# Edge rows gathered as pairs from a DRAM table built during the sort, results kept in place, bias products limited to the sort steps

## The chip, the cores and the metric

The kernel runs on one core of one Trainium2 chip. The metric is the device time of one execution in microseconds (us), as the median of several runs. The engines are TensorE (PE in the profile), VectorE (DVE), ScalarE (ACT), GpSimd (POOL) and SyncE (SP); SP's queue issues the plain DMAs and POOL's queue the indirect ones.

## The reference

A graph layer with residual and layer norm, on 50,000 nodes of 128 features and 12,500 edges of 128 features. `src` is drawn at random and unsorted.

```python
edge_sum = jax.ops.segment_sum(edge_attr, src, num_segments=50000)
inputs = jnp.concatenate([x, edge_sum], axis=1)          # 50000 x 256
h = jax.nn.elu(inputs @ W0 + b0)                         # W0 256 x 128
h = jax.nn.elu(h @ W2 + b2)                              # W2 128 x 128
y = x + h @ W3 + b3                                      # W3 128 x 128
m = jnp.mean(y, axis=-1, keepdims=True)
v = jnp.var(y, axis=-1, keepdims=True)
out = (y - m) / jnp.sqrt(v + 1e-05)
```

Everything is float32.

## The kernel before, in words

**Items.** The work is 124 items, numbered c. Items 0 to 97 (ND = 98) are dense: 512 nodes each, computed as if no edge touched them, and stored whole by plain DMAs. Items 98 to 122 (NE = 25, group g) are the edge items: 500 sorted edges each, as 4 columns of 125. Each takes the rows of x that its edges' sources name, adds the summed edge features in layer 1, and scatters its 500 result rows over what the dense items stored (rows that are not a node's last edge go out of bounds and are dropped). Item 123 (LAST) mends the sums that cross a column's end. So no scatter may start before all dense rows are stored.

**Steps.** Every engine walks the same steps c = 0 to 128, and in step c works on several items at once. TensorE: layer 1 of item c-1 (L487, for edge items also L498 with the sums), for edge items the transposes of x's rows (`turn`, L512), layer 2 of item c-2 (L519), layer 3 of item c-3 (L531 and L532, four blocks). ScalarE: exp of layer 1 (L591), the biased copy of x (L585), exp of layer 2 (L591), then `squares` of item c-3 (L600, L605, L607), whose result `seed` VectorE needs. VectorE: `root` of item c-4 (L832 to L838, waits for `seed`), elu of layer 1 (L819, L822), `normalise` of item c-4 (L850, its end counts `o_ready`), elu of layer 2. Each engine's queue is in order.

**Bias products.** Where `fused(s, layer)` holds, TensorE adds the bias by a short bf16 product (`add_bias`, L479), and VectorE's elu is one instruction (L815) and not two (L819, L822). It holds for both layers in the sort's steps 3 to 19, and for layer 2 in every even step from 20 to 98.

**Sort.** VectorE sorts the edges by source between its other work in steps 1 to 19 (KEY_AT = 20). SP then sends words and keys through DRAM. From step 21 POOL knows the sorted edge numbers (`edge_i`) and sources (`key_i`).

**Gathers.** POOL issues 4 indirect DMAs for the features of group g (L369, 125 rows of 512 bytes each) and 4 for its rows of x (L375), 200 in all; `pace` spreads them over the dense items by waiting on `o_ready`.

**Sums.** In steps 95 to 119 (`SUMS`, group g in step 95 + g) TensorE multiplies the features by 0/1 masks (`sums`, L463, four products, one behind each part of its step), and ScalarE copies the sum out of PSUM (`copy_sums`, L574) at the end of its step, behind `squares`. The first product of the next group waits for that copy (`sum_ready`). VectorE makes the masks (L788) of the next group from `keyB`, the keys of one group spread over 128 partitions.

**SP's order.** In step c SP issues the load of item c+3, then waits for `o_ready` of item c-4 and stores it if it is dense. In steps 95 to 115 it also issues `load_keys(g+4)` (L322), which waits until the masks of group g are made, since `keyB` has four slots.

**End.** When SP's stores have landed (POOL itself waits on the four `stored` semaphores), POOL scatters: 4 indirect DMAs for each edge item (L391), each item when `o_ready` says so, and one for LAST (L384).

Of the kernel before, what the change touches and what calls it, by code (L numbers as in the profile page):

```python
# [12 lines left out]
P = 128  # L13
J = 4
# [9 lines left out]
def gnn_resnorm(nc, x, src, attr, W0, b0, W2, b2, W3, b3, x_items, word_rows, key_rows, out):  # L24
# [22 lines left out]
    LAST = ND + NE  # L47
    NI = LAST + 1
    SLOTS = 4
    SUM_SLOTS = 5  # L50
    AHEAD = 3

# [27 lines left out]
    KEY_AT = SORT_AT + len(GROUPS)  # L80
    SUM_LEAD = 3
    SUMS = {ND - SUM_LEAD + g: g for g in range(NE)}
# [3 lines left out]
    assert KEY_AT + 2 < min(SUMS) and END_AT <= LAST  # L86

    with ExitStack() as ctx:
# [76 lines left out]
        attr_edge = sb("attr_edge", [P, EC, P])  # L165
        x_edge = sb("x_edge", [P, EC, P])
# [70 lines left out]
        attr_got = [sem(f"attr_got{k}") for k in range(SLOTS)]  # L237
        x_got = [sem(f"x_got{k}") for k in range(SLOTS)]
        x_loaded = [sem(f"x_loaded{k}") for k in range(SLOTS)]
        stored = [sem(f"stored{k}") for k in range(SLOTS)]  # L240
        scattered = [sem(f"scattered{k}") for k in range(SLOTS)]

        DENSE_ON = [len(range(k, ND, SLOTS)) for k in range(SLOTS)]
# [9 lines left out]
        def is_dense(c):  # L253
            return c < ND
# [6 lines left out]

        def scatters(c):

            return 16 * sum(blocks(k) for k in range(ND, c + 1) if k % SLOTS == c % SLOTS)
# [26 lines left out]
        def _(sp):  # L291
# [9 lines left out]
            def rows_of(ap, c):  # L301
                first = N - ROWS if c == ND - 1 else c * ROWS
                return ap[first:first + ROWS, :].rearrange("(p j) f -> p (j f)", p=P)

            def load(c):
                if not is_dense(c):
                    return
                k = c % SLOTS
                at_least(sp, xT_ready, c - SLOTS + 1)
                sp.dma_start(x_sb[:, k, :], x_items[c * P:(c + 1) * P, :]).then_inc(x_loaded[k], 16)  # L310

            def store(c):
                sp.wait_ge(o_ready, c + 1)
                if c == ND - 1:

                    sp.wait_ge(stored[(c - 1) % SLOTS], 16 * DENSE_ON[(c - 1) % SLOTS])
                sp.dma_start(rows_of(out, c), o_sb[:, c % SLOTS, :]).then_inc(stored[c % SLOTS], 16)
# [10 lines left out]
            for c in range(STEPS_END):  # L328
# [5 lines left out]
                load(c + AHEAD)  # L334
                if 0 <= c - 4 < ND:
                    store(c - 4)
# [9 lines left out]
            for k in range(SLOTS):  # L346
                sp.wait_ge(stored[k], 16 * DENSE_ON[k])

        @block.gpsimd
        def _(pool):  # L350
# [6 lines left out]
            def pace(half):  # L357

                first = KEY_AT - 1
                pool.wait_ge(o_ready, first + half * (ND - 6 - first) // (2 * NE))  # L360

            def gather(g):
                k = g % SLOTS
                pace(2 * g)
                if g >= SLOTS:
                    pool.wait_ge(attr_got[k], got(g - SLOTS))
                    pool.wait_ge(x_got[k], got(g - SLOTS))
                for c in range(J * g, J * g + J):
                    nc.gpsimd.indirect_dma_start(  # L369
                        out=attr_edge[0:EP, c, :], out_offset=None, in_=attr[:, :],  # L370
                        in_offset=bass.IndirectOffsetOnAxis(ap=edge_i[0:EP, c:c + 1], axis=0),
                    ).then_inc(attr_got[k], 16)
                pace(2 * g + 1)
                for c in range(J * g, J * g + J):
                    nc.gpsimd.indirect_dma_start(  # L375
                        out=x_edge[0:EP, c, :], out_offset=None, in_=x[:, :],
                        in_offset=bass.IndirectOffsetOnAxis(ap=key_i[0:EP, c:c + 1], axis=0),
                    ).then_inc(x_got[k], 16)

            def scatter_out(c):  # L380
                k = c % SLOTS
# [544 lines left out]
```

## Time and profile before

| | before |
|---|---|
| median of 3 runs | 605.97 us (605.18 to 607.83) |
| the profiled execution, its own time | 606.39 us |
| its span, first to last instruction | 604.3 us |
| TensorE busy | 544.3 us, 90% |
| VectorE busy | 466.1 us, 77% |
| ScalarE busy | 439.7 us, 73% |
| GpSimd busy | 371.9 us, 62% |
| DMA bytes | 77.84 MB, mean 129 GB/s |

The span leaves 606.39 - 604.3 = 2.1 us of the execution outside. Busy shares are means over stages that differ: the sort (to some 108 us), the dense steps (to some 395 us), the steps with sums (to some 550 us), and a tail. A wait matters only where the waiting engine sets the time of its stage.

### The profile page before, as it was taken

To read this page: it belongs to the slowest core of one execution; us is meant where nothing else is said; L and a number is where in the kernel's file an instruction comes from. 1 tells how busy PE (TensorE), PEld (TensorE's weight loads), DVE (VectorE), ACT (ScalarE), POOL (GpSimd) and SP (SyncE) were. 2 spreads that over 40 slices of the span, in tenths; PEclk is the share of its full clock that TensorE was granted. 3 is DMA by queue.
4 is the path that set the end of the run, shared out by engine and by line. 5 is a ranking of instruction groups with operands and counts; after the bars stand their busy time and mean duration, and the time that the engine had idled before them with its cause. 6 is when DMAs were issued, how large, how long until landed. Compare 5 with 4: busy or idle time off the path is not lost.

```text
span 604.3 us, 10977 instructions
## 1 busy us (share of the span) xinstructions
PE 544.3 (90%) x2930; PEld 360.4 (60%) x2930; DVE 466.1 (77%) x1348; ACT 439.7 (73%) x1632; POOL 371.9 (62%) x310
## 2 busy tenths in 40 slices
PE   3999999999999999999999999989999999997930
PEld 1455555566666666666666666666667666665620
DVE  5988899988888888888888888877678676776640
ACT  2577767888888888888888988876665666665630
POOL 0000000377887787788778778877157777777676
PEclk9999999999999999999999999999999999999985
DMA  3134332486666655555665656554422332211111
GB/s 111 49 109 120 121 106 91 144 245 184 183 180 183 180 175 179 178 174 175 181 180 183 175 174 179 173 153 117 112 77 76 82 79 71 71 38 37 34 39 34
DMA packets 57451, 77.84 MB, mean 129 GB/s; under 512 B 22590, under 2 KB 27782, under 8 KB 57390
## 3 DMA queue, kind: packets, MB, share of 16 engines
q1 hardware_dynamic: 33294, 58.26, 31.7%
q0 software_dynamic: 24096, 18.89, 12.7%
q8 instruction: 24, 0.39, 0.3%
q14 instruction: 37, 0.30, 0.2%
HBM read 45.30 MB, written 32.24 MB: 128 GB/s over the span
## 4 chain that ended last, share of the span: by engine, by line
PE 82%; DVE 9%; issue 5%; POOL 2%; ACT 1%; SPq 0%; DMA 0%; DVEq 0%; POOLq 0%
PE z_ps L531 18%; PE z_ps L532 17%; PE l_ps L519 17%; PE l_ps L487 16%; PE sum_ps L463 5%; PE l_ps L498 4%; PE l_ps L479 3%; PE turn_ps L512 2%; POOL out_dram L391 2%; DVE h L815 2%; DVE net L721 2%; DVE o_sb L850 1%; DVE net L720 1%; PE turn_ps L435 1%; DVE e L819 0%
## 5 line engine op out<-in xcount | busy, mean ns | idle before, releaser
L369 POOL DMA_INDIRECT attr_edge<-in_edge_attr_dram,edge_i x100 | 124.8, 1248 | 143.9 <-issue 141.1
L531 PE MATMUL z_ps<-center,xT 128*128 128x128 f32 (+1 forms) x986 | 194.7, 279 | 8.5 <-issue 6.4
L600 ACT ACTIVATE sq<-z_ps 128x128 f32<-128x128 f32 (+1 forms) x493 | 129.8, 278 | 94.7 <-PE z_ps L532 93.7
L532 PE MATMUL z_ps<-w3c,h 128*128 128x128 f32 (+1 forms) x986 | 190.1, 274 | 0.0
L531 PEld LDWEIGHTS z_ps<-center,xT 128*128 128x128 f32 (+1 forms) x986 | 152.3, 191 | 41.5 <-issue 36.3
L391 POOL DMA_INDIRECT out_dram<-o_sb,target_i x100 | 119.9, 1199 | 53.5 <-issue 49.3
L532 PEld LDWEIGHTS z_ps<-w3c,h 128*128 128x128 f32 (+1 forms) x986 | 149.0, 191 | 0.0
L375 POOL DMA_INDIRECT x_edge<-in_x_dram,key_i x100 | 124.3, 1243 | 30.5 <-issue 28.1
L822 DVE SCALAR_TENSOR_TENSOR h<-l_ps,neg_bias,e 128x512 f32<-128x512 f32 (+2 forms) x174 | 129.2, 742 | 6.2
L519 PE MATMUL l_ps<-h,w 128*128 128x512 f32 (+1 forms) x248 | 130.0, 606 | 1.8 <-DVE h L822 1.8
L591 ACT ACTIVATE e<-l_ps,bias 128x512 f32<-128x512 f32 (+2 forms) x174 | 116.7, 671 | 18.7 <-issue 5.3
L487 PE MATMUL l_ps<-xT,w0x 128*128 128x512 f32 (+1 forms) x248 | 128.8, 601 | 1.2 <-ACT xT L585 1.2
L600 ACT ACTIVATION_READ_ACCUMULATOR sq<-z_ps 128x1 f32 (+1 forms) x493 | 102.0, 207 | 0.0
L819 DVE TENSOR_SCALAR e<-e,bias 128x512 f32<-128x512 f32 (+2 forms) x174 | 95.6, 550 | 3.8 <-issue 2.5
L850 DVE TENSOR_TENSOR o_sb<-z_ps,rstd 128x512 f32<-128x512 f32 (+1 forms) x124 | 84.1, 678 | 0.1
L585 ACT ACTIVATE xT<-x_sb,bias_x 128x512 f32<-128x512 f32 x98 | 69.8, 712 | 7.6 <-DVE neg_bias L668 7.6
L519 PEld LDWEIGHTS l_ps<-h,w 128*128 128x128 f32 x248 | 43.7, 192 | 44.1 <-issue 29.8
L463 PEld LDWEIGHTS sum_ps<-same,attr_edge 125*128 125x128 f32 x200 | 31.8, 190 | 42.9 <-issue 41.7
L832 DVE SCALAR_TENSOR_TENSOR newton<-seed 128x4 f32<-128x4 f32 (+1 forms) x124 | 20.7, 167 | 45.1 <-ACT seed L607 44.3
L591 ACT ACTIVATE e<-l_ps,minus_one 128x512 f32<-128x512 f32 x74 | 49.9, 675 | 4.4 <-PE l_ps L479 3.8
L463 PE MATMUL sum_ps<-same,attr_edge 125*128 125x125 f32 x200 | 39.9, 283 | 12.7 <-issue 12.7
L815 DVE SCALAR_TENSOR_TENSOR h<-e,l_ps 128x512 f32<-128x512 f32 x74 | 50.2, 679 | 0.0
(126 smaller groups left out, 402.5 us busy)
## 6 DMA issues: line engine op xcount, KB each, us to landing
x_sb<-x_items_dram SPq DMA_DIRECT2D x98, 256.0 KB
out_dram<-o_sb SPq DMA_DIRECT2D x98, 256.0 KB
keyB<-key_rows_dram SPq DMA_DIRECT2D x25, 250.0 KB
attr_edge<-in_edge_attr_dram,edge_i POOLq DMA_INDIRECT x100
x_edge<-in_x_dram,key_i POOLq DMA_INDIRECT x100
out_dram<-o_sb,target_i POOLq DMA_INDIRECT x100
w<-in_L_gnn_W_dram SPq DMA_DIRECT2D x2, 64.0 KB, 1.9
w0x<-in_L_gnn_W_dram SPq DMA_DIRECT2D x1, 64.0 KB, 2.1
```

What stands on the lines that cost most here:

```text
L369: nc.gpsimd.indirect_dma_start(out=attr_edge[0:EP, c, :], out_offset=None, in_=attr[:, :], in_offset=bass.IndirectOffsetOnAxis(ap=edge_i[0 ...
L375: nc.gpsimd.indirect_dma_start(out=x_edge[0:EP, c, :], out_offset=None, in_=x[:, :], in_offset=bass.IndirectOffsetOnAxis(ap=key_i[0:EP, c: ...
L391: nc.gpsimd.indirect_dma_start(out=out[:, :], out_offset=bass.IndirectOffsetOnAxis(ap=target_i[0:EP, col:col + 1], axis=0), in_=o_sb[0:EP, ...
L463: T.matmul(sum_ps[:, j * EP:(j + 1) * EP], attr_edge[0:EP, c, :], same[0:EP, c % (2 * J), :], start=True, stop=True).then_inc(same_free, 1)
L487: mm = T.matmul(ps, w0x[:], xT[:, c % SLOTS, 0:n], start=True, stop=alone)
L519: mm = T.matmul(l2_ps[c % 2][:, 0:n], w2[:], h1[:, c % 2, 0:n], start=True, stop=not fused(s, 2))
L531: T.matmul(z, xT[:, c % SLOTS, j * q:(j + 1) * q], center[:], start=True, stop=False)
L532: mm = T.matmul(z, h2[:, c % 2, j * q:(j + 1) * q], w3c[:], start=False, stop=True)
L591: A.activation(e[:, c % 2, 0:n], ps[:, 0:n], ACT.Exp, bias=bias[:, 0:1]).then_inc(done, 1)
L600: t = A.activation(sq[0:q, j, :], z_ps[c % 2][0:q, j * P:(j + 1) * P], ACT.Square, scale=float(P) ** -0.5, accum_out=ssq[0:q, c % 2, j:j + 1])
L819: V.tensor_scalar(e[:, c % 2, 0:n], e[:, c % 2, 0:n], 1.0, bias[:, 0:1], ALU.min, ALU.add).then_inc(min_ready, 1)
L822: V.scalar_tensor_tensor(out=h[:, c % 2, 0:n], in0=ps[:, 0:n], scalar=neg_bias[:, 0:1], in1=e[:, c % 2, 0:n], op0=ALU.max, op1=ALU.add).th ...
```

## The change

Five things change.

1. While VectorE sorts, a table `pairs` of 12,500 rows of 256 floats is built in DRAM: the row of x of the edge's source in the left half, the edge's features in the right. POOL fetches the x rows of the unsorted edges (`fetch_x`, 100 indirect DMAs, starting as soon as `src` is in), SP writes them to the table (`pair_x`, 25 DMAs in steps 2, 3, 5, 6, ... 38) and copies the features from DRAM to DRAM (`pair_attr`, 25 DMAs in steps 2 to 26).
2. After the sort POOL gathers pairs, 100 indirect DMAs of 125 rows of 1024 bytes in place of 200 of 512 bytes, without `pace`, once all 25 pieces of both halves have landed.
3. `normalise` writes an edge item's rows over its x rows in `pair_edge`, and the scatters read them there; the wait for earlier scatters is gone.
4. POOL waits for one count, `dense_out`, in place of the four `stored` semaphores. SP raises it by one for each dense item (`confirm`): for item d-2 behind the store of item d, and for items 96 and 97 behind the last step of its loop.
5. `fused` holds only in steps 3 to 19. `sums` puts two products behind layer 1 and two behind `turn`. `copy_sums` stands ahead of `squares`.

```diff
+    PAIR_X = {2 + 3 * g // 2: g for g in range(NE)}
+    PAIR_ATTR = {2 + g: g for g in range(NE)}
...
         def fused(s, layer):
-            if s < KEY_AT:
-                return FUSED_FROM <= s
-            return layer == 2 and s % 2 == 0 and is_dense(s - 2)
+            return FUSED_FROM <= s < KEY_AT
...
+            def confirm(d):
+                sp.wait_ge(stored[d % SLOTS], 16 * (d // SLOTS + 1))
+                sp.sem_inc(dense_out, 1)
+
+            def pair_x(g):
+                k = g % SLOTS
+                sp.wait_ge(x_fetched[k], 16 * J * (g // SLOTS + 1))
+                sp.dma_start(pairs.rearrange("(p c) f -> p c f", p=EP)[:, J * g:J * g + J, 0:P],
+                             x_early[0:EP, k, :, :]).then_inc(x_paired[k], 16)
+
+            def pair_attr(g):
+                last = min(E, ROWS * (g + 1))
+                sp.dma_start(pairs[ROWS * g:last, P:2 * P], attr[ROWS * g:last, :]).then_inc(attr_paired, 16)
...
+                if item_in(c - 4) and is_dense(c - 4):
+                    d = ITEMS[c - 4][1]
+                    store(d)
+                    if d >= 2:
+                        confirm(d - 2)
+                if c in PAIR_ATTR:
+                    pair_attr(PAIR_ATTR[c])
+                if c in PAIR_X:
+                    pair_x(PAIR_X[c])
...
                 if c in SUMS and SUMS[c] + SLOTS < NE:
                     load_keys(SUMS[c] + SLOTS)
-            for k in range(SLOTS):
-                sp.wait_ge(stored[k], 16 * DENSE_ON[k])
+            confirm(ND - 2)
+            confirm(ND - 1)
...
+            def fetch_x(g):
+                k = g % SLOTS
+                at_least(pool, x_paired[k], 16 * (g // SLOTS))
+                for j in range(J):
+                    nc.gpsimd.indirect_dma_start(
+                        out=x_early[0:EP, k, j, :], out_offset=None, in_=x[:, :],
+                        in_offset=bass.IndirectOffsetOnAxis(ap=src_i[0:EP, J * g + j:J * g + j + 1], axis=0),
+                    ).then_inc(x_fetched[k], 16)
...
+            pool.wait_ge(src_loaded, 16)
+            for g in range(NE):
+                fetch_x(g)
+            for k in range(SLOTS):
+                pool.wait_ge(x_paired[k], 16 * len(range(k, NE, SLOTS)))
+            pool.wait_ge(attr_paired, 16 * NE)
             pool.wait_ge(edge_ready, 1)
             for g in range(NE):
                 gather(g)
...
             pool.wait_ge(target_ready, 1)
-            for k in range(SLOTS):
-                pool.wait_ge(stored[k], 16 * DENSE_ON[k])
-            for c in range(ND, NI):
-                scatter_out(c)
+            pool.wait_ge(dense_out, ND)
+            for g in range(NE):
+                scatter_out(g)
...
-                return [one(j) for j in range(J)]
+                return [some(0), some(1)]
...
+                if c in SUMS:
+                    parts.append(lambda: copy_sums(SUMS[c]))
                 if item_in(c - 3):
                     parts.append(lambda: squares(c - 3))
                 run(parts, [])
-                if c in SUMS:
-                    copy_sums(SUMS[c])
...
+                elif kind == "edge":
+                    rows_out = pair_edge[0:EP, J * n:J * n + J, 0:P]
```

SP's queue at its end, before the change (the last dense stores, then `load_keys` L322 alone; the last row is the end, with its waits for the stores):

```order
L317 DMA out_dram<-o_sb 128x512 [waits o_ready]
L322 DMA keyB<-key_rows_dram 128x500 [waits same_ready]
L317 DMA out_dram<-o_sb 128x512 [waits stored0,o_ready]
L322 DMA keyB<-key_rows_dram 128x500 [waits same_ready] x15
L88 UNCONDITIONAL_BRANCH [waits stored2,stored3,stored1,stored0]
```

The same place after the change. The two waits on the last row are those of `confirm(96)` and `confirm(97)`, which raise `dense_out` to 98:

```order
L341 DMA keyB<-key_rows_dram 128x500 [waits stored2,same_ready]
L321 DMA out_dram<-o_sb 128x512 [waits stored0,o_ready]
L341 DMA keyB<-key_rows_dram 128x500 [waits stored3,same_ready]
L341 DMA keyB<-key_rows_dram 128x500 [waits same_ready] x14
L100 UNCONDITIONAL_BRANCH [waits stored0,stored1]
```

The last loads of keys (15 before, and 15 after in two rows) stood behind the last dense store before and still do; what moved is that the count which releases POOL is now raised behind them. POOL's queue after the change, from the last gather of pairs (L398) over the row for LAST (L421) to the first scatters (L406), shows who waits:

```order
L398 DMA pair_edge<-pairs_dram,edge_i 125x256 x3
L421 DMA x_end<-in_x_dram,end_i 100x128 [waits ends_ready]
L406 DMA out_dram<-pair_edge,target_i 50000x128 [waits o_ready,dense_out,target_ready]
L406 DMA out_dram<-pair_edge,target_i 50000x128 x3
L406 DMA out_dram<-pair_edge,target_i 50000x128 [waits o_ready]
```

The first scatter waits for `dense_out`, and all others are queued behind it.

TensorE in one step with sums, before the change (L463 are the products of the sums, L512 the transposes of `turn`):

```order
L498 MATMUL l_ps<-sumT,w0e 128x500 [waits sum_ready]
L463 MATMUL sum_ps<-same,attr_edge 128x125 [waits same_ready,sum_ready,attr_got3]
L512 MATMUL turn_ps<-ident,x_edge 128x125 [waits xT_ready,x_got0]
L512 MATMUL turn_ps<-ident,x_edge 128x125 x3
L463 MATMUL sum_ps<-same,attr_edge 128x125 [waits same_ready]
L519 MATMUL l_ps<-h,w 128x500 [waits h2_ready,h1_ready]
L463 MATMUL sum_ps<-same,attr_edge 128x125 [waits same_ready]
L531 MATMUL z_ps<-center,xT 125x128 [waits o_ready,h2_ready]
```

And ScalarE in the same step before, from the copy at a step's end on:

```order
L574 COPY sumT<-sum_ps 128x500 [waits parts_ready,l1_ready,same_free]
L591 ACTIVATE e<-l_ps,bias 128x500 [waits h1_ready,l1_ready]
L585 ACTIVATE xT<-turn_ps,bias_x 128x500 [waits z_ready,turn_ready]
L591 ACTIVATE e<-l_ps,bias 128x500 [waits h2_ready,l2_ready]
L600 ACTIVATE sq,ssq<-z_ps 125x128 [waits ssq_ready,rstd_ready,z_ready]
L600 ACTIVATE sq,ssq<-z_ps 125x128 x3
L605 ACTIVATE seed<-ssq,eps 125x4 [waits ssq_ready]
L607 ACTIVATE seed<-seed 125x4 [waits log_ready]
```

TensorE after the change, the same step:

```order
L523 MATMUL l_ps<-sumT,w0e 128x500 [waits sum_ready]
L488 MATMUL sum_ps<-same,pair_edge 128x125 [waits same_ready,sum_ready,pair_got3]
L488 MATMUL sum_ps<-same,pair_edge 128x125 [waits same_ready]
L537 MATMUL turn_ps<-ident,pair_edge 128x125 [waits xT_ready,pair_got0]
L537 MATMUL turn_ps<-ident,pair_edge 128x125 x3
L488 MATMUL sum_ps<-same,pair_edge 128x125 [waits same_ready] x2
L544 MATMUL l_ps<-h,w 128x500 [waits h2_ready,h1_ready]
L556 MATMUL z_ps<-center,xT 125x128 [waits o_ready,h2_ready]
```

ScalarE after it:

```order
L599 COPY sumT<-sum_ps 128x500 [waits parts_ready,l1_ready,same_free]
L626 ACTIVATE sq,ssq<-z_ps 125x128 [waits ssq_ready,rstd_ready,z_ready]
L626 ACTIVATE sq,ssq<-z_ps 125x128 x3
L631 ACTIVATE seed<-ssq,eps 125x4 [waits ssq_ready]
L633 ACTIVATE seed<-seed 125x4 [waits log_ready]
L617 ACTIVATE e<-l_ps,bias 128x500 [waits h1_ready,l1_ready]
```

All four products now stand ahead of layers 2 and 3, and the copy stands ahead of `squares`, which waits for layer 3.

## Rows read from the trace of the kernel before

**Rows 1.** Page: span, TensorE's busy time, the chain that ended last

```profile
span 604.3 us, 10977 instructions
PE 544.3 (90%) x2930; PEld 360.4 (60%) x2930; DVE 466.1 (77%) x1348; ACT 439.7 (73%) x1632; POOL 371.9 (62%) x310
PE 82%; DVE 9%; issue 5%; POOL 2%; ACT 1%; SPq 0%; DMA 0%; DVEq 0%; POOLq 0%
```

**Rows 2.** L322 (SP's loads of keys): ns min/median/max, first and last start us

```profile
L322 SPq DMA_DIRECT2D keyB<-key_rows_dram x25: 319/320/655, 123.8 to 518.3; - x25
```

**Rows 3.** L391 (POOL's scatters), and POOL's last two: start us, us, operation

```profile
L391 POOL DMA_INDIRECT out_dram<-o_sb,target_i x100: 1186/1190/1407, 443.0 to 598.5; - x100
...
598.49 1.19 POOL L391 DMA_INDIRECT out_dram<-o_sb,target_i  x1 [0.30 <-issue]
599.98 0.99 POOL L384 DMA_INDIRECT out_dram<-o_sb,end_i  x1 [0.30 <-issue]
```

**Rows 4.** Timeline: VectorE's L850 for items 17, 90, 98 and 110

```profile
108.56 0.68 DVE L850 TENSOR_TENSOR o_sb<-z_ps,rstd 128x512 f32<-128x512 f32 x1
...
394.61 0.68 DVE L850 TENSOR_TENSOR o_sb<-z_ps,rstd 128x512 f32<-128x512 f32 x1
...
441.23 0.69 DVE L850 TENSOR_TENSOR o_sb<-z_ps,rstd 125x512 f32<-125x512 f32 x1
...
516.03 0.68 DVE L850 TENSOR_TENSOR o_sb<-z_ps,rstd 125x512 f32<-125x512 f32 x1
```

**Rows 5.** Source view of POOL's gathers of features, L369

```profile
L369 POOL DMA_INDIRECT attr_edge<-in_edge_attr_dram,edge_i x100: 1208/1212/1427, 115.2 to 417.8; - x100
```

**Rows 6.** Timeline of two dense steps: the rows of one loop through three engines

```profile
247.18 0.28 ACT L600 ACTIVATE sq<-z_ps 128x128 f32<-128x128 f32 x1 [0.79 <-PE z_ps L532]
...
248.92 0.17 DVE L832 SCALAR_TENSOR_TENSOR newton<-seed 128x4 f32<-128x4 f32 x1 [1.05 <-ACT seed L607]
...
252.05 0.75 DVE L822 SCALAR_TENSOR_TENSOR h<-l_ps,neg_bias,e 128x512 f32<-128x512 f32 x1
...
252.85 0.49 PE L531 MATMUL z_ps<-center,xT 128*128 128x128 f32 x2 [0.17 <-issue]
...
254.94 0.28 ACT L600 ACTIVATE sq<-z_ps 128x128 f32<-128x128 f32 x1 [0.79 <-PE z_ps L532]
```

**Rows 7.** The chain, same steps: start us, us, what

```profile
250.65 0.86 PE l_ps L487 x2
251.50 0.86 PE l_ps L519 x2
252.36 0.32 PE l_ps L479
252.68 0.17 issue
252.85 0.49 PE z_ps L531 x2
253.34 0.22 PE z_ps L532 x2
```

**Rows 8.** Timeline of a step with sums: the copy and the product behind it

```profile
480.56 1.01 PE L487 MATMUL l_ps<-xT,w0x 128*128 128x500 f32 x2
...
482.16 0.56 ACT L574 COPY sumT<-sum_ps 128x500 f32<-128x500 f32 x1
...
482.82 0.46 PE L463 MATMUL sum_ps<-same,attr_edge 125*128 125x125 f32 x2 [0.41 <-issue]
...
486.79 1.01 PE L487 MATMUL l_ps<-xT,w0x 128*128 128x500 f32 x2
```

**Rows 9.** Windows: us, busy PE, PEld, DVE, ACT, POOL, clock, DMA share, GB/s

```profile
60.00:90.00 30.00, 29.30 (x150) 16.96 (x150) 27.31 (x120) 21.91 (x81) 0.00 (x0) 1.00 0.38 119
...
120.00:135.00 15.00, 14.62 (x82) 10.15 (x82) 12.57 (x31) 11.73 (x47) 12.26 (x10) 1.00 0.82 244
```

**Rows 10.** DMA queues: POOL's queue, packets, MB, share of 16 engines

```profile
q0 software_dynamic: 24096, 18.89, 12.7%
```

More of the change, by code:

```diff
@@ L51, in gnn_resnorm @@
     AHEAD = 3
+    ITEMS = [("dense", d) for d in range(ND)] + [("edge", g) for g in range(NE)]
+    LAST = len(ITEMS)
+    ITEMS.append(("last", 0))
+    NI = len(ITEMS)
+    DENSE_AT = [c for c in range(NI) if ITEMS[c][0] == "dense"]
+    EDGE_AT = [c for c in range(NI) if ITEMS[c][0] == "edge"]
+    assert [ITEMS[c][1] for c in DENSE_AT] == list(range(ND)) and [ITEMS[c][1] for c in EDGE_AT] == list(range(NE))
     LOG = 7
@@ L80, in gnn_resnorm @@
     KEY_AT = SORT_AT + len(GROUPS)
+    PAIR_X = {2 + 3 * g // 2: g for g in range(NE)}
+    PAIR_ATTR = {2 + g: g for g in range(NE)}
     SUM_LEAD = 3
-    SUMS = {ND - SUM_LEAD + g: g for g in range(NE)}
+    SUMS = {EDGE_AT[g] - SUM_LEAD: g for g in range(NE)}
     END_AT = max(SUMS) + 2
@@ L85, in gnn_resnorm @@
     FUSED_FROM = 3
-    assert KEY_AT + 2 < min(SUMS) and END_AT <= LAST
+    assert max(PAIR_X) + 4 < min(SUMS) and KEY_AT + 5 < min(SUMS) and END_AT <= LAST
     with ExitStack() as ctx:
@@ L253, in is_dense @@
         def is_dense(c):
-            return c < ND
+            return ITEMS[c][0] == "dense"
         def item_in(c):
@@ L404, in _ @@
             pool.wait_ge(target_ready, 1)
-            for k in range(SLOTS):
-                pool.wait_ge(stored[k], 16 * DENSE_ON[k])
-            for c in range(ND, NI):
-                scatter_out(c)
-            for c in range(NI - SLOTS, NI):
-                pool.wait_ge(scattered[c % SLOTS], scatters(c))
+            pool.wait_ge(dense_out, ND)
+            for g in range(NE):
+                scatter_out(g)
+            pool.wait_ge(o_ready, LAST + 1)
+            nc.gpsimd.indirect_dma_start(
+                out=out[:, :], out_offset=bass.IndirectOffsetOnAxis(ap=end_i[0:EC, 1:2], axis=0),
+                in_=x_end[0:EC, :], in_offset=None, bounds_check=N - 1, oob_is_err=False,
+            ).then_inc(scattered, 16)
+            pool.wait_ge(scattered, 16 * (EC + 1))
         @block.tensor
@@ L455, in sums, with some @@
             def sums(g):
-                def one(j):
+                def some(half):
                     def do():
-                        c = J * g + j
-                        if j == 0:
-                            pe.wait_ge(attr_got[g % SLOTS], got(g))
+                        if half == 0:
+                            pe.wait_ge(pair_got[g % SLOTS], got(g))
                             at_least(pe, sum_ready, g)
-                        pe.wait_ge(same_ready, c + 1)
-                        T.matmul(sum_ps[:, j * EP:(j + 1) * EP], attr_edge[0:EP, c, :], same[0:EP, c % (2 * J), :],
-                                 start=True, stop=True).then_inc(same_free, 1)
+                        for j in range(2 * half, 2 * half + 2):
+                            c = J * g + j
+                            pe.wait_ge(same_ready, c + 1)
+                            T.matmul(sum_ps[:, j * EP:(j + 1) * EP], pair_edge[0:EP, c, P:2 * P], same[0:EP, c % (2 * J), :],
+                                     start=True, stop=True).then_inc(same_free, 1)
                     return do
@@ L510, in turn @@
                 for j in range(blocks(c)):
-                    rows_in = x_end[0:q, :] if c == LAST else x_edge[0:q, J * (c - ND) + j, :]
+                    rows_in = x_end[0:q, :] if c == LAST else pair_edge[0:q, J * ITEMS[c][1] + j, 0:P]
                     mm = T.transpose(turn_ps[:, j * q:(j + 1) * q], rows_in, ident[0:q, 0:q])
```

114 lines of the change are left out of this document (46 added, 68 removed).

## The prediction

> **What bounds the kernel now.** I read the page first. TensorE is busy 90% of the 604.3 us span and the chain that ended last runs over it for 82% [rows 1], so TensorE, or a loop that contains it, sets most of the time. The exception is the end. POOL's scatters start at 443.0, the last of item 122 at 598.49 and LAST's at 599.98, 1.49 us apart, without a wait for anything but issue [rows 3]. The reader should see there that 100 such scatters need 100 x 1.49 = 149 us, whatever the other engines do, and that they begin right behind the dense stores. Third I read SP's row of key loads: the last is issued at 518.3 [rows 2], 75 us after the scatters began. Last the timelines of a dense step and of a step with sums, for the loops through several engines.
>
> **The release of the scatters.** The edit that decides is the fourth. Before, POOL itself waited for the stores. After, it waits for `dense_out` = 98, and the last two counts are raised by SP behind its whole loop, behind `load_keys(24)`. That load waits until the masks of group 20 are made, in step 114. Before, nobody waited for SP there; now the first scatter does, and behind it in POOL's queue all 101. In the old schedule the load goes out at 518.3 and takes 0.3, so the release would come at 518.6 [rows 2]. Item 98's output ended at 441.23 + 0.69 = 441.9 and the first scatter began at 443.0 [rows 3, 4]: 1.1 us from release to scatter. So with all else unmoved: 518.6 + 1.1 + 149 + 0.99 for LAST + 3.3 from its end (600.97) to the span's end (604.3) = 673.0. Compute ends long before (LAST's rows come near 585 or earlier), so nothing hides this, and everything that the change gains counts only up to step 114. The scatter itself costs what it did: 125 rows of 512 bytes, another source tile. Bounds of its pace: 1.49, or 1.71 if each took the longest 1.41 beside busy engines; 40 of them run beside compute, and the median of 1.19 over all, most of them beside compute [rows 3], speaks for 1.49.
>
> **Dense steps: bias products.** 37 of the 40 products removed lie in steps 20 to 94. In the chain one costs 0.32, and 0.17 of issue and a first block of 0.49 where the next takes 0.22 follow it [rows 7]: 0.76 us, or 37 x 0.76 = 28 us if TensorE alone set the steps. I do not believe that. Follow the loop [rows 6]: ScalarE starts its squares at 247.18, VectorE's root begins on their result at 248.92 (+1.74), VectorE works without a pause to the end of L822 at 252.80 (+3.88), TensorE starts layer 3 at 252.85, and the squares after it start at 254.94 (+2.09). That closes in 7.76 us for two steps, and items 17 to 90 came every (394.61 - 108.56) / 73 = 3.92 us [rows 4], 7.84 for two. So the pair is set by the step in which VectorE has both elus in two instructions; the step with the bias product is the one with slack. After the change both kinds of steps are the long kind, and both loops close in 7.76, or 7.49 if a block's restart (0.27) goes. VectorE alone needs 3.55 to 3.88 a step. I take 3.85 where it was 3.92: 75 x 0.07 = 5 us gained. Bounds: 28 gained (above), 5 lost if two tight loops disturb each other.
>
> **Steps with sums.** Before, the copy out of PSUM starts at 482.16, behind the squares, and TensorE's first product of the next group at 482.82, after a wait of 0.41 [rows 8]. Layer 3, squares, copy and the next product form a loop of one step, and the step is 486.79 - 480.56 = 6.23 us [rows 8]. After, the copy no longer waits for layer 3. TensorE's own work is then 3 x 0.86 for the wide products, 8 x 0.22 in layer 3, 4 x 0.22 for the sums and 0.44 for the transposes = 5.66, by the pieces of [rows 7], so 0.57 less in each of 16 steps, 9 us. Steps 95 to 98 still hold dense items and little else and can gain another 3. Together 12 us before step 114; bounds 5 (half of it is lost to restarts) and 14.
>
> **The sort, and the table.** POOL was idle there. A gather takes 1.21 [rows 5] and with the issue gap of 0.3 some 1.5, so `fetch_x` needs 150 us; `pair_x(24)` goes out in step 38, near 108.6 + 17 x 3.9 = 175 us [rows 4]. The pair gathers then run from 180 to some 335, and the first sum needs them near 385: hidden, with 50 us to spare. If that cover went, each us late would be a us. The traffic: pieces of 256 KB, of x fetched every 6 us and written every 7.1, of features copied once a step of 4.8, add 43 + 36 + 55 = 134 GB/s to 119, that is 253 [rows 9]. The stretch 120 to 135 moved 244 GB/s at a share of 0.82 with TensorE busy 97% [rows 9]. So I take 2 us. Lower bound 0; the upper one is the third rival. SP's extra issues (50 in 36 steps, at some 0.4 each) lie in its waits. Halving POOL's gathers after the sort gains nothing, since they were hidden.
>
> **The sum.** 673.0 - 5 - 12 + 2 = 658 us of span. The profiled execution had 2.1 us outside its span, 606.39 in all, 0.4 above the median of the runs: 658 + 2.1 - 0.4 = 660 us.
>
> **The rivals.**
>
> 1. *TensorE alone bounds the dense steps.* For it: the chain names TensorE only. Against: the loop above. The 28 us come off in full instead of 5: 637. Chance 0.1.
>
> 2. *The count is not late* (the other side). If `dense_out` were full when the last dense store lands, the first scatter would start near 443.0 - 5 - 3 = 435 and the end be 435 + 149 + 0.99 + 3.3 + 2.1 - 0.4 = 590: faster by 2.6%. It is one mechanism: the place of the last two `confirm`. The point from which it decides is a release at 606 - 156 = 450 us; the key load stands at 518.3 before the gains of 15 us [rows 2]. The queue order leaves no way around it, unless I misread what that load waits for. Chance 0.03.
>
> 3. *The table's traffic stretches the sort.* `pair_x` has 125 partitions. If its 256,000 bytes went over only 5 of the 16 engines, each would get 51 KB. POOL's queue moved 18.89 MB in 12.7% of 16 x 604.3 us, 15.4 KB a us and engine [rows 10], so 3.3 us each. On those engines the shares in the sort are 0.38 as before [rows 9], 0.22 for the features (1.06 of 4.8 us), 0.17 for the fetch and 3.3 / 7.1 = 0.46: 1.23, and as much up to step 38. Over 180 us that overfills by up to 28 us, and loads and stores in SP's queue come late with it: 686. Spread over all 16 it is 0.91, and the 2 us above hold. The trace has no row of a single engine; a mean share of 0.38 is no proof that 1.23 would be needed. Chance 0.17. The Trainium skill states it, in "DMA: Bandwidth & Descriptors", "Why a DMA increments its semaphore by 16 and not by 1": a transfer runs on the largest number of engines, at most 16, that divides the sizes of both slowest dimensions, for 125 that is 5. By that rule alone the sum would be 686, by the rows of the mean share 660; but the page's own figure of about 27 GB/s for an engine would leave room for it. No row here shows either.
>
> **How the numbers follow.** My forecast has 0.68 (range of its own 650 to 670), the rivals 0.1, 0.03 and 0.17, and 0.02 is for what I do not see. A range that leaves out 2 in 10 must reach toward the third rival, whose middle is 675: 644 to 680. A measurement of this kernel tells 0.5% from no change, 3 us. Only the second rival is not slower: slower 0.96, same 0.01, faster 0.03.
>
> **What would show it.** After: the last key load near 500 us, the first scatter 1 to 2 us behind it and no scatter before; some 100 scatters 1.49 apart with TensorE idle in the last 90 us; dense steps of 3.8 to 3.9 without alternation; steps with sums of 5.7; the copy ahead of the squares; pair gathers from 180 to 335; item 17 near 109 us. I am wrong if scatters begin near 440, if the dense steps fall to 3.5, or if item 17 comes later than 115.

## The result, and the profile after

| | before | after |
|---|---|---|
| median | 605.76 us (605.18 to 607.83, 4 runs) | 674.02 us (672.65 to 678.45, 4 runs) |
| ratio | 1 | 1.1134, 95% interval 1.1106 to 1.1163 |
| span of the profiled execution | 604.3 us | 670.9 us |

The kernel is 68 us slower. The page of the changed kernel: span, busy times, two of the slices, the chain that ended last.

```profile
span 670.9 us, 11033 instructions
...
PE 529.9 (79%) x2890; PEld 358.4 (53%) x2890; DVE 483.5 (72%) x1388; ACT 439.2 (65%) x1632; POOL 372.5 (56%) x310
...
PE   3999998889999999999999999999999969200000
...
POOL 7866676657728888888880000000004777778676
...
PE 37%; DVE 19%; issue 15%; POOL 12%; ACT 10%; DMA 4%; another core or an unknown queue 2%; SPq 1%; POOLq 0%; ACTq 0%; DVEq 0%
```

A slice is 16.8 us. TensorE is idle in the last five, and POOL stands idle in nine slices while all others work; then it runs alone to the end. In [rows 1] TensorE carried 82% of the chain, here 37%. The source view of SP's last key load and of POOL's scatters, and the timeline of the hand-over, which answer to [rows 2, 3]:

```profile
L341 SPq DMA_DIRECT2D keyB<-key_rows_dram x25: 319/320/2834, 132.2 to 509.8; - x25
```

```profile
L406 POOL DMA_INDIRECT out_dram<-pair_edge,target_i x100: 1185/1189/1332, 511.3 to 664.7; - x100
```

```profile
509.82 0.32 SPq L341 DMA_DIRECT2D keyB<-key_rows_dram  x1
...
511.30 1.33 POOL L406 DMA_INDIRECT out_dram<-pair_edge,target_i  x1 [157.24 <-issue]
...
666.15 0.99 POOL L430 DMA_INDIRECT out_dram<-x_end,end_i  x1 [0.30 <-issue]
```

The load ends at 510.1 and the first scatter begins 1.2 us later. POOL had been idle for 157 us; the releaser reads "issue", so the profile names nobody for this wait; what released POOL has to be read from the code and from SP's row. From 511.3 to LAST's row at 666.15 are 154.9 us for 100 scatters, 1.55 each.

VectorE's output of an item is the kernel's clock; its starts (for item 98 and 110 the edge rows) in us, before against after, with the differences over each stretch:

| item | before | after | stretch | before | after |
|---|---|---|---|---|---|
| 30 | 161.18 | 168.07 | start to 30 | 161.18 | 168.07 |
| 90 | 394.61 | 401.62 | 30 to 90 | 233.43 | 233.55 |
| 98 | 441.23 | 440.53 | 90 to 98 | 46.62 | 38.91 |
| 110 | 516.03 | 507.56 | 98 to 110 | 74.80 | 67.03 |

So the first 30 items cost 6.9 us, the 60 dense ones gained nothing, and the steps with sums gained 15.5 us. All of it counts only through the release of POOL. A few us of one trace are not a result by themselves: four kernels below that run the same code up to step 19 (the changed one, e1, e2, e4) have item 17 at 112.72, 115.09, 111.38 and 109.57.

The two dense steps in the timeline after, to hold against [rows 6]:

```profile
256.56 0.49 PE L556 MATMUL z_ps<-center,xT 128*128 128x128 f32 x2 [0.57 <-DVE h L848]
...
258.64 0.28 ACT L626 ACTIVATE sq<-z_ps 128x128 f32<-128x128 f32 x1 [0.87 <-PE z_ps L557]
...
260.38 0.16 DVE L858 SCALAR_TENSOR_TENSOR newton<-seed 128x4 f32<-128x4 f32 x1 [0.46 <-ACT seed L633]
...
263.57 0.75 DVE L848 SCALAR_TENSOR_TENSOR h<-l_ps,neg_bias,e 128x512 f32<-128x512 f32 x1
264.38 0.49 PE L556 MATMUL z_ps<-center,xT 128*128 128x128 f32 x2 [0.54 <-DVE h L848]
```

The bias product is gone, and in its place TensorE waits 0.57 and 0.54 us for VectorE's `h`. The pair takes 264.38 - 256.56 = 7.82 us, as before (7.76 to 7.84).

### The profile page after: what moved, and what is told of

Its sections match the earlier page's. It is cut to its first block, busy times and chain, and to the rows that moved or that the text cites. A ratio compares the mean times of both kernels' runs of the same rounds, so it can differ in the third digit from the quotient of the medians.

```text
span 670.9 us, 11033 instructions
## 1 busy us (share of the span) xinstructions
PE 529.9 (79%) x2890; PEld 358.4 (53%) x2890; DVE 483.5 (72%) x1388; ACT 439.2 (65%) x1632; POOL 372.5 (56%) x310
## 4 chain that ended last, share of the span: by engine, by line
PE 37%; DVE 19%; issue 15%; POOL 12%; ACT 10%; DMA 4%; another core or an unknown queue 2%; SPq 1%; POOLq 0%; ACTq 0%; DVEq 0%
PE z_ps L556 10%; PE z_ps L557 9%; POOL out_dram L406 9%; ACT sq L626 6%; PE l_ps L544 5%; DVE e L845 5%; PE l_ps L512 5%; DVE h L848 4%; PE sum_ps L488 3%; POOL x_early L388 3%; PE l_ps L523 3%; ACT seed L631 2%; DMA pairs_dram<-x_early 2%; PE turn_ps L537 1%
## 5 line engine op out<-in xcount | busy, mean ns | idle before, releaser
L406 POOL DMA_INDIRECT out_dram<-pair_edge,target_i x100 | 119.3, 1193 | 192.5 <-issue 191.9
L848 DVE SCALAR_TENSOR_TENSOR h<-l_ps,neg_bias,e 128x512 f32<-128x512 f32 (+1 forms) x214 | 159.1, 744 | 7.6
L617 ACT ACTIVATE e<-l_ps,bias 128x512 f32<-128x512 f32 (+1 forms) x214 | 143.4, 670 | 24.4 <-PE l_ps L544 13.3
L388 POOL DMA_INDIRECT x_early<-in_x_dram,src_i x100 | 123.7, 1237 | 57.4 <-DMA pairs_dram<-x_early 28.1
L398 POOL DMA_INDIRECT pair_edge<-pairs_dram,edge_i x100 | 126.5, 1265 | 43.4 <-issue 30.2
L512 PE MATMUL l_ps<-xT,w0x 128*128 128x512 f32 (+1 forms) x248 | 130.4, 608 | 6.3 <-ACT xT L611 4.7
L845 DVE TENSOR_SCALAR e<-e,bias 128x512 f32<-128x512 f32 (+1 forms) x214 | 111.4, 521 | 8.3 <-ACT e L617 4.4
L879 DVE TENSOR_TENSOR o_sb<-z_ps,rstd 128x512 f32<-128x512 f32 x98 | 66.7, 681 | 0.0
L858 DVE SCALAR_TENSOR_TENSOR newton<-seed 128x4 f32<-128x4 f32 (+1 forms) x124 | 19.7, 159 | 58.7 <-ACT seed L633 43.5
L512 PEld LDWEIGHTS l_ps<-xT,w0x 128*128 128x128 f32 x248 | 38.6, 196 | 9.0 <-ACT xT L611 5.9
L631 ACT ACTIVATE seed<-ssq,eps 128x4 f32<-128x4 f32 (+1 forms) x124 | 36.8, 297 | 4.0
L488 PE MATMUL sum_ps<-same,pair_edge 125*128 125x125 f32 x200 | 31.2, 276 | 0.6 <-issue 0.3
```

Of the source, the lines that this page charges most:

```text
L388: nc.gpsimd.indirect_dma_start(out=x_early[0:EP, k, j, :], out_offset=None, in_=x[:, :], in_offset=bass.IndirectOffsetOnAxis(ap=src_i[0:EP ...
L398: nc.gpsimd.indirect_dma_start(out=pair_edge[0:EP, c, :], out_offset=None, in_=pairs[:, :], in_offset=bass.IndirectOffsetOnAxis(ap=edge_i[ ...
L406: nc.gpsimd.indirect_dma_start(out=out[:, :], out_offset=bass.IndirectOffsetOnAxis(ap=target_i[0:EP, c:c + 1], axis=0), in_=pair_edge[0:EP ...
L488: T.matmul(sum_ps[:, j * EP:(j + 1) * EP], pair_edge[0:EP, c, P:2 * P], same[0:EP, c % (2 * J), :], start=True, stop=True).then_inc(same_f ...
L512: mm = T.matmul(ps, w0x[:], xT[:, c % SLOTS, 0:n], start=True, stop=alone)
L617: A.activation(e[:, c % 2, 0:n], ps[:, 0:n], ACT.Exp, bias=bias[:, 0:1]).then_inc(done, 1)
```

## The experiments

Ratios are against the kernel before, run beside each experiment; its median was 604.48 us beside e1 to e4, 603.66 beside e5 to e8, 605.50 beside e9 to e11 and 604.64 beside e12. Between these groups the ratios are the safer measure.

**e1: the count is raised early.** The changed kernel, with the last two counts raised in step 102, ahead of that step's key load:

```diff
+                if c == ND + 4:
+                    confirm(ND - 2)
+                    confirm(ND - 1)
                 if c in SUMS and SUMS[c] + SLOTS < NE:
                     load_keys(SUMS[c] + SLOTS)
-            confirm(ND - 2)
-            confirm(ND - 1)
```

> The changed kernel with the last two counts raised at the top of step 102, right behind the last dense store's step, and not behind SP's whole loop. My theory (the late count costs all of the loss): the dense rows land near 441, the first scatter starts near 442.5, and from there to the end it takes what it took in the changed kernel, 670.9 - 511.3 = 159.6 us: span 602, 605 us. Rival (the table or the pair gathers also cost something behind the release): the span stays above 620.

Measured: 604.79 us, ratio 0.9998 (0.9978 to 1.0019), span 604.3. The source view of its scatters:

```profile
L407 POOL DMA_INDIRECT out_dram<-pair_edge,target_i x100: 1185/1189/1354, 443.8 to 598.1; - x100
```

The whole loss is gone by moving two lines. What else the change does adds up to nothing in the time; e3 and what follows show that this nothing is a gain and a loss.

**e2: the same lines in step 108.** A dose between the two: `if c == ND + 10`, the rest as in e1.

> The changed kernel with the last two counts raised at the top of step 108, behind the key loads for group 16 (which wait for the masks of group 12). My theory: the release follows that load, near 465, and the end follows the release by the same 160.8 us (510.1 to 670.9): span 626, 629 us. Rival (the late end has another cause, such as the queue's depth or the source tile of the scatters): no change from 674, or a time not in line with the release.

Measured: 627.15 us, ratio 1.0377 (1.0345 to 1.0408), span 625.9.

```profile
L407 POOL DMA_INDIRECT out_dram<-pair_edge,target_i x100: 1185/1188/1417, 465.4 to 619.7; - x100
```

First scatter at 443.8, 465.4 and 511.3 in e1, e2 and the changed kernel; from there to the end of the span 160.5, 160.5 and 159.6 us. The time is the release and a constant.

**e3: the sums' part alone.** The kernel before, with two products behind layer 1 and two behind `turn`, and the copy ahead of `squares`:

```diff
-                return [one(j) for j in range(J)]
+                return [some(0), some(1)]
...
+                if c in SUMS:
+                    parts.append(lambda: copy_sums(SUMS[c]))
                 if item_in(c - 3):
                     parts.append(lambda: squares(c - 3))
                 run(parts, [])
-                if c in SUMS:
-                    copy_sums(SUMS[c])
```

> The kernel before with one part of the change: two products of the sums behind layer 1 and two behind the transposes, and the copy ahead of the squares. My theory (one loop per step through layer 3, squares, copy and the first product): steps with sums fall from 6.25 to 5.6 us, item 98 ends 7.5 us earlier, the first scatter starts near 435.5 and the scatters, now behind compute all the time, end the span near 597: 599 us, 1.1% faster. Rival (VectorE or TensorE holds the step at 6.2 anyway): 606, steps of 6.2.

Measured: 595.72 us, ratio 0.9851 (0.981 to 0.9892). Item 98 at 435.08 against 441.23, and its first scatter at 436.8 against 443.0: the 6 us by which the dense items end earlier. From there to the end of the span it takes 158.1 us, against 604.3 - 443.0 = 161.3 before, so another 3 us come from behind item 98. Before, an item of four scatters had to wait for its rows, which came every 6.23 us, where four scatters need 4 x 1.49 = 5.96. The first scatter of item 99 in the kernel before shows it:

```profile
447.51 1.24 POOL L391 DMA_INDIRECT out_dram<-o_sb,target_i  x1 [0.30 <-issue]
449.20 1.19 POOL L391 DMA_INDIRECT out_dram<-o_sb,target_i  x1 [0.45 <-issue]
```

Item 99's output ends at 448.29, about 1 us ahead of that scatter, as with item 98. In e3 items 98 to 110 come every 6.02 us (5.6 was expected), and most of these waits are gone.

**e4: bias products back.** e1 with `fused` as before.

> e1_confirm_early with the bias products of the even steps put back (40 more products, the one other difference). My theory (a loop of VectorE, layer 3 and squares sets two dense steps): item 90 ends within 2 us of e1, the time is within 2 us of e1. Rival (TensorE alone sets the dense steps, and the gain was hidden by the table's traffic): item 90 ends some 28 us later and the time is some 28 us longer than e1.

Measured: 603.71 us, ratio 1.0005 (0.9976 to 1.0034). Items 30 to 90 took 233.1 us (e1 232.3). The 40 products cost nothing in the time. Item 90 came 4.2 us earlier than in e1, not within 2; but at item 17, up to where the two kernels run the same code, it was 5.5 us ahead already.

**e5: bias products out, without the table.** e3 with `fused` as in the change.

> e3 (the kernel before with the new order of sums and copy) without the bias products of the even steps: no table, the old gathers. My theory (the loop sets the dense steps): items 30 to 90 take 233 us as in e3, the time is within 2 us of e3, 596. Rival (the products cost TensorE 0.76 each, and the table's traffic hid that gain in the changed kernel): item 90 ends up to 28 us earlier, 570.

Measured: 596.6 us, ratio 0.9868 (0.9841 to 0.9895), the same as e3. Its item 30 comes at 162.62 and item 98 at 438.07, and items 30 to 90 took 235.5 us where 233 was expected: without the products the dense steps are, if anything, longer. Its scatters:

```profile
L389 POOL DMA_INDIRECT out_dram<-o_sb,target_i x100: 1185/1189/1393, 439.8 to 588.9; - x100
```

These 100 start 149.1 / 99 = 1.51 us apart. In e1 it was 154.3 / 99 = 1.56; this difference is taken up below.

**e6 and e7: VectorE's output behind layer 2.** In e6 (e3 otherwise, products kept) and e7 (e5 otherwise, without them), to shorten VectorE's part of the loop:

```diff
-                run([scale, first_layer, output, second_layer], beside)
+                run([scale, first_layer, second_layer, output], beside)
```

> e3 with VectorE's output of item c-4 put behind the elu of layer 2 instead of ahead of it, bias products of the even steps kept. My theory: the loop through VectorE gets 0.6 shorter (7.16 for two steps), but TensorE with one product in two steps needs 2 x 3.51 + 0.76 = 7.78, so the steps stay at 3.9: within 3 us of e3. Rival (VectorE's order is without effect on any bound): the same; a gain of over 8 us would speak against the price of 0.76.

> e6 without the bias products of the even steps. My theory: the loop is 7.16 for two steps and TensorE needs 7.02, VectorE 3.55 to 3.7 a step, so dense steps take some 3.65 and not 3.89: item 90 ends some 18 us earlier than in e3, and the tail of scatters with it: 578. Rival (VectorE or ScalarE alone holds 3.9 once all steps have two-instruction elus): 595, as e3.

Measured: e6 591.94 us, ratio 0.978 (0.9748 to 0.9812), the best of all kernels here, 3.8 us below e3 where at most 3 was expected; e7 596.24, ratio 0.9863 (0.9836 to 0.989), where 578 was expected. The windows of e6 show TensorE without a gap:

```profile
200.00:250.00 50.00, 49.88 (x274) 33.92 (x274) 41.82 (x99) 44.70 (x173) 39.94 (x34) 1.00 0.64 183
```

In e7, one of two steps shows what the sum had missed:

```profile
256.09 0.68 DVE L849 TENSOR_TENSOR o_sb<-z_ps,rstd 128x512 f32<-128x512 f32 x1
...
256.92 0.46 PE L530 MATMUL z_ps<-center,xT 128*128 128x128 f32 x2 [0.51 <-DVE o_sb L849]
```

Layer 3 writes into one of two `z_ps` buffers, and it waits until the output has read the older one. With the output last and without the products, two steps still take 7.76 us; with the products (e6) they take 7.58. As a reading of this row: a missing bias product gives TensorE 0.5 us only to wait; where the product stands, it fills that wait and makes VectorE's step shorter by an instruction. In this order the products are a gain (items 30 to 90 in 228.0 us against 233.3), where in the old order they made no difference.

**e8: the table's x half in two transfers.** e1, with `pair_x` cut into 112 and 13 partitions; the same bytes. POOL's two waits for these transfers count 32 a piece in place of 16 (left out here).

```diff
-                sp.dma_start(pairs.rearrange("(p c) f -> p c f", p=EP)[:, J * g:J * g + J, 0:P],
-                             x_early[0:EP, k, :, :]).then_inc(x_paired[k], 16)
+                for low, high in ((0, 112), (112, EP)):
+                    sp.dma_start(pairs.rearrange("(p c) f -> p c f", p=EP)[low:high, J * g:J * g + J, 0:P],
+                                 x_early[low:high, k, :, :]).then_inc(x_paired[k], 16)
```

> e1_confirm_early with each DMA that writes x rows into the table cut into one of 112 partitions and one of 13. Theory of the third rival (125 partitions go over 5 of the 16 engines, and that delays the table and what stands behind it): POOL's waits for these DMAs (28 us in 8 waits, and 13 before the first pair gather) fall below 8 and 5, item 17 ends near 109 to 110, the time is 0 to 4 us below e1. Rival (the sheer bytes of the table slow the sort): waits, item 17 (110 to 115) and time as in e1.

Measured: 599.27 us, ratio 0.9916 (0.9886 to 0.9947), 5.5 us below e1 (0.8% by the ratios; the slowest run of e8, 600.55, is below the fastest of e1, 601.61). Item 17 at 109.82 against 115.09, item 30 at 163.35 against 170.82. POOL's waits for these transfers fell from 30.8 us in e1 to 19.7, and the one before the first gather of pairs from 12.3 to 8.1; below 8 and below 5 were expected. SP's queue in the timeline, first of e1, then of e8:

```profile
103.85 0.62 SPq L331 DMA_DIRECT2D pairs_dram<-x_early  x1
104.52 2.71 SPq L314 DMA_DIRECT2D x_sb<-x_items_dram  x1
```

```profile
98.80 1.17 SPq L332 DMA_DIRECT2D pairs_dram<-x_early  x2
100.01 0.40 SPq L314 DMA_DIRECT2D x_sb<-x_items_dram  x1
```

Behind a `pair_x` of 125 partitions, the issue of the next load holds SP for 2.71 us; behind the two pieces for 0.40. Over all 23 loads that stand right behind a `pair_x`, the median is 2.92 us in the changed kernel and 0.44 in e8. The stretch 60 to 90 us in windows, first of the changed kernel, then of e8:

```profile
60.00:90.00 30.00, 29.28 (x143) 16.27 (x143) 26.66 (x113) 21.73 (x87) 20.50 (x18) 1.00 0.82 230
```

```profile
60.00:90.00 30.00, 29.24 (x143) 16.23 (x143) 27.02 (x117) 21.80 (x83) 19.79 (x18) 1.00 0.83 240
```

The mean share of the engines and the bytes are the same or higher, so more traffic is not what made e1 slower than e8. That the slow issues made it is not shown: e4 has them too (median 3.17) and its item 17 at 109.57, as early as e8's.

**e9, e10, e11: VectorE's root behind layer 1.** With `run([first_layer, scale, output, second_layer], beside)`, in e5 (e9), e3 (e10) and e8 (e11), to take the root out of the loop of [rows 6].

> e3 without the bias products of the even steps, and with VectorE's root of item c-4 moved from ahead of the elu of layer 1 to behind it. e7 had put the output, which layer 3 waits for too (two z buffers), in the place of the elu in the same loop: 3.81 of VectorE either way. Here the wait for the seed stands behind 1.2 us of other work, so the loop loses 1.2 us of its 7.76. My theory, mended: TensorE needs 3.51 a step and VectorE 3.55 to 3.65, dense steps of 3.6; items 30 to 90 take 216 and not 233, the end moves 20 to 23 us: 573 to 576. Rival (VectorE at 3.9 a step by its own work, or ScalarE at 3.5 with its waits): 595.

> e9 with the bias products of the even steps kept. In e6 TensorE ran without a gap, and two steps took 7.59 = 2 x 3.51 + 0.57. My theory: the same here, 3.80 a step, 592 us; so the products cost nothing as long as the loop stands (e4, e5) and some 0.2 a step, 15 to 20 us in all, once it is gone. Rival (products free of cost): as e9.

> The whole change with three mends: the last two counts raised in step 102 (e1), the writes of x rows cut in 112 and 13 partitions (e8), root behind the elu of layer 1 (e9). My theory: e8's 599 less the 20 to 23 us of the dense steps: 577 to 580, so the table still costs some 3 us against e9 and brings nothing. Rival (with half the gathers VectorE and POOL disturb each other less, so it ends ahead of e9): 570.

Measured: e9 619.43 us, ratio 1.0229 (1.0183 to 1.0275); e10 618.79, ratio 1.0228 (1.0197 to 1.0258); e11 625.58, ratio 1.0354 (1.0298 to 1.0411). All three went the wrong way. A row of e9:

```profile
253.09 0.52 DVE L818 TENSOR_SCALAR e<-e,bias 128x512 f32<-128x512 f32 x1 [0.75 <-ACT e L590]
```

VectorE now stands still for ScalarE's exp of layer 1. ScalarE is in order: that exp comes behind the squares and the seed. The root had used this wait; behind the elu it became 0.6 us of work in the loop. By this row the last link of the loop into VectorE is the exp, not the seed.

**e12: all together.** e8 with the bias products back and e6's order.

> The changed kernel with the count raised early and the table written in two transfers (599.27 us), its even-step bias products put back, and VectorE's order in a dense step as in the best version of the kernel before: scale, first layer, second layer, output (591.94 us there, against 595.72 us with the output ahead of the second layer, both with the products kept). If the loop of the dense steps sets the middle here as it does there, the pair of dense steps falls from 7.8 to 7.6 us with 30 to 40 pairs behind it, so 599.3 less 4 to 7 us: 593 to 595 us, and the table of pairs is then a cost of 1 to 3 us that buys nothing. Rival: 100 gathers fewer relieve the dense steps once TensorE bounds them, and the time is 590 us or less.

Measured: 602.98 us (600.69 to 604.43, 10 runs), ratio 0.9968 (0.995 to 0.9986): 3.7 us slower than e8, where 5 faster was expected. Item 17 comes at 112.29 (e8 109.82), items 30 to 90 take 230.8 us (e8 232.6, e6 228.0), and 90 to 98 take 41.3 (e8 38.9, e6 41.9). So against e8 this kernel gains 1.8 us in the dense steps and loses 2.4 behind item 90, 2.5 by item 17 and 0.5 from there to item 30. Item 16 still stands where it stood (106.47 against 106.39). In the next step a row of the timeline has TensorE waiting for the sorted words:

```profile
111.63 0.35 PE L468 MATMUL turn_ps<-ident,words 100*125 100x100 f32 x1 [2.31 <-DMA words<-word_rows_dram]
```

In e8 the same wait is 0.41. The transfer took about as long in both, 2.9 us from its issue to this row against 2.6, so the row says where the step lost time and not that the table's traffic did it. Both expectations failed. Against e6, which has no table, this kernel is 1.9% slower.

## Why the prediction was right in direction and 14 us short

**How much of it was luck.** The main mechanism was forecast and is shown. The number 660 was 14 us short, and the forecast's own range of 650 to 670 missed 674. The stated 644 to 680 holds it only because it was stretched toward the third rival, which did not come at its size. The misses also cancelled in part: 4.9 us more in the sort, 5.1 less gained in the dense steps and 5.9 more in the scatters, against 3.5 more gained in the steps with sums.

**The release of the scatters: right.** The last key load, the first scatter 1.2 us behind it, no scatter before, TensorE idle in the last five slices, 84 us: all as forecast, and e1 and e2 show by dose that this alone makes the 68 us. The second rival (the count is not late) fell with it; its 590 would have needed more than an early count, since e1, which makes the count early, gives 604.8: the first scatter there starts at 443.8 and not at 435. The release came at 510.1 and not at 518.6 - 15 = 503.6, and the scatters took 154.9 us and not 149. The span's miss of 670.9 - 658 = 12.9 us is these 6.5 and 5.9 and 0.5 elsewhere.

**Dense steps: a loop and not TensorE alone, as forecast; the gain and one link wrong.** The forecast of 5 us rested on a pair of 7.84 falling to 7.70; it stayed at 7.8 (30 to 90: 233.55 against 233.43). No gain came, and e4 against e1 and e5 against e3 show the same in two other kernels. The first rival (28 us off if TensorE sets the steps) is refuted. (The count of products in it is off by one: the even steps 20 to 94 are 38.) The forecast of dense steps "without alternation" failed too: they alternate at 4.09 and 3.73 us without a bias product in either. e7 showed layer 3 waiting for one of two `z_ps` buffers; that the loop closes over the pair for that reason is a reading of it, and was not tried. The link from the seed to VectorE's root, which the prediction's loop went over, is not what holds it: e9 took the root out of it and the steps grew to 4.19 us. The step of the prediction that failed here is the gain of 0.07 us a step. It was measured from the 3.92 of items 17 to 90, but items 30 to 90 came every 3.89 already, and with the products gone TensorE waited for `h` and the pair stayed as long.

**Steps with sums: right in mechanism, sized too small.** 5.59 us a step over items 98 to 110 (67.03 / 12) against 6.23, where 5.66 was forecast; between items 90 and 98 7.7 us were gained and not 3. Together that is 15.5 us, just beyond the bound of 14. The late count may help here, since no scatter ran beside these steps. In e2 the items come every 5.58 to 5.60 us from 98 until two steps behind its first scatter, and then every 4.6 to 7.1; items 98 to 110 took 70.0 us in e1, 70.7 in e2, 72.2 in e3 and 68.5 in e4, but 67.0 to 67.4 in e5 to e8, which have scatters there too. What disturbs the steps in the first four is not shown. The copy at 474.69 stands ahead of the next step's first product, which no longer waits:

```profile
474.69 0.57 ACT L599 COPY sumT<-sum_ps 128x500 f32<-128x500 f32 x1
...
475.66 1.00 PE L512 MATMUL l_ps<-xT,w0x 128*128 128x500 f32 x2
```

**The sort and the table: 6.9 us, not 2.** This is the third rival's place, at a quarter of its size. The time went to 674 by the first mechanism with this one added, not to the rival's 686. Item 17 came at 112.72, where near 109 was forecast. The rival's own sum does not give its 28 us either: a load of 1.23 over 180 us is 0.23 x 180 = 41 us too much. How the 6.9 us divide can be read only roughly, since single traces differ by as much. By item 30, against the kernel of the same order and bias products without the table, the table costs 4.4, 5.5 and 8.2 us (e2 at 166.99, the changed kernel at 168.07, e1 at 170.82, against e5's 162.62) and 4.7 (e4 against e3). With the transfer cut it costs 0.7 (e8 against e5), 3.5 (e12 against e6) and 4.7 (e11 against e9). So the cut helps or does nothing, and part of the cost stays with it. Against the kernel before, the removed products of steps 20 to 30 are in the 6.9 as well: e5's item 30 is 1.5 us behind e3's. POOL's waits in the changed kernel show the fetches and the first gather of pairs held up by the same transfers:

```profile
POOL x_early L388 <- DMA pairs_dram<-x_early: 28.1, 8, 6.3
POOL pair_edge L398 <- DMA pairs_dram<-x_early: 13.3, 1, 13.3
```

The gathers of pairs so ran from 195.9 to 352.5 and not from 180 to 335, still ahead of the first sum. That a transfer of 125 partitions runs on few engines, as the Trainium skill has it in "DMA: Bandwidth & Descriptors", "Why a DMA increments its semaphore by 16 and not by 1", fits e8 in one point: 112 is a multiple of 16, and the slow issues behind the transfer are gone. It fits less well that POOL's waits fell only by a third. The rule by itself does not give the rival's 28 us; that took the rate of 15.4 KB a us and engine of [rows 10] as well, and the two together are refuted by the 6.9 us. No row shows a single engine, so how many engines worked stays open.

**The scatters' pace: 1.55, not 1.49.** The median is 1.19 + 0.30 as forecast. Of the 5.9 us above it, 5.2 are two pauses. The timeline of POOL around the second:

```profile
629.08 1.19 POOL L406 DMA_INDIRECT out_dram<-pair_edge,target_i  x1 [0.30 <-issue]
633.27 1.19 POOL L406 DMA_INDIRECT out_dram<-pair_edge,target_i  x1 [3.01 <-issue]
```

4.19 us from one to the next where 1.49 is the rule, and 3.95 from 568.27 to 572.22. They stand ahead of the 40th and the 79th scatter, and they stand ahead of the same two in every kernel with the table (e1, e2, e4, e8, e11 and e12 too), wherever these fall between 498 and 633 us. In the kernels without the table they are missing: e5, e6, e7, e9 and e10 have no gap above 2.3 us, and the two each in the kernel before and in e3 (61st and 77th, 57th and 77th) lie at an item's first scatter. So the forecast that "the scatter itself costs what it did" failed: the change makes them 5 us longer than they are without it (e5). Which part of it does is open. The table kernels scatter from `pair_edge` and not from `o_sb`, count all scatters on one semaphore and not on four, and have gathered rows of 1024 bytes before; none of the three was tried alone.

**The whole change, mended.** With the count early and the transfer cut (e8) it takes 599.27 us; the kernel before with the sums' part alone (e3) takes 595.72, and with VectorE's output last (e6) 591.94. The table, the pairs and the bias products' removal together buy nothing. By the ratios the table kernels are 1.3% and 1.6% slower than the same kernel without the table (e1 against e5, e4 against e3), and with the transfer cut 0.5%, 1.2% and 1.9% (e8 against e5, e11 against e9, e12 against e6); the two pauses are in each of these. How to shorten the loop of the dense steps stays open: e7 has a row that points to the two `z_ps` buffers, e9 one that points to ScalarE's exp, and a third buffer was not tried.

## What to carry to other kernels

When one engine's count releases another, look at what stands ahead of the count in its queue, not at what the count means: the dense rows were stored in time for a first scatter at 443.8 us (e1), and the changed kernel reported them at 510, behind loads of keys that have nothing to do with them. If a loop through three engines sets a step, work taken off one of them only becomes a wait; list every wait that closes the loop (here a free buffer and an in-order exp) before pricing a new order, because e7 and e9 each failed on a link that was not listed. And try each part of a bundled change by itself: here the new order of sums and copy held the gain (e3, 1.5%), the place of two counts a loss of 68 us, and the table a smaller loss that the gain hid. Last, look at the same event in kernels with and without the change before calling it noise or a habit of the engine: the scatters' two pauses come with the table.

## What the runs showed of the hardware

- Behind one `pair_x` of 125 partitions and 250 KB, the issue of SP's next load takes 0.3 to 5.1 us, median 2.92, in the changed kernel; behind the same bytes cut as 112 and 13 partitions 0.35 to 1.33, median 0.44, in e8. Where no table is written (the kernel before) the median issue of such a load is 0.43. The kernel with the cut is 5.5 us faster (e8 against e1); that the issues are the reason is not shown.
- An indirect gather of 125 rows holds POOL for 1.21 us at 512 bytes a row [rows 5] and at 1024 bytes, in the source view of the changed kernel:

```profile
L398 POOL DMA_INDIRECT pair_edge<-pairs_dram,edge_i x100: 1207/1212/1475, 195.9 to 351.3; - x100
```

- In all seven kernels with the table, POOL's scatters pause for an extra 2.4 to 2.8 us ahead of the 40th and of the 79th of 100; in the seven without it they do not. The cause is open.
- TensorE's granted clock was 1.00 through the dense steps; once TensorE idles in the tail of the changed kernel the slices of the page show 0.5, that is 1.2 of its 2.4 GHz. No time hangs on that, since POOL alone works there.
